# X, Z and V of a long convolution: planes moved between partitions inside SBUF, V summed by TensorE, keys set aside and spread later

## What is computed

```python
dtA = exp(log_dt) * (-exp(log_A_real) + 1j * A_imag)          # (256, 64)
Ct = C * (exp(dtA) - 1) / A
K = 2 * real(einsum('hn,hnl->hl', Ct, exp(dtA[:, :, None] * arange(1024))))
y = irfft(rfft(x, n=2048) * rfft(K, n=2048).T)[:, :1024]      # long convolution
x = layernorm(x + layernorm_affine(x + y + x * D))
x = layernorm(x + cross_attention(x, ctx))                    # 16 heads of 16
x = layernorm(x + dense_gate(x) + experts(x))                 # 4 heads, 8 of 1024 experts
```

## Time and profile before

| | us |
|---|---|
| median of 3 runs | 710.08 (703.44 to 712.31) |
| profiled execution, own time | 702.58 |
| its span, first to last instruction | 700.8 |
| first matmul of `conv` after the start | 188.22 |
| busy: TensorE, VectorE, ScalarE, GpSimd | 590.3, 506.6, 404.9, 279.9 |

### The profile page before, as it was taken

How to read it: one execution, slowest core, us unless ns; L and a number is a source line. 1 busy time by engine, 2 the same in 40 slices (tenths; PEclk the granted TensorE clock), 3 DMA queues, 4 the chain that set the end, 5 groups by cost and what they waited for, 6 DMA issues and landing times.

```text
span 700.8 us, 9712 instructions
## 1 busy us (share of the span) xinstructions
PE 590.3 (84%) x3132; PEld 383.4 (55%) x3132; DVE 506.6 (72%) x1046; ACT 404.9 (58%) x593; POOL 279.9 (40%) x333
## 2 busy tenths in 40 slices
PE   5743587785296778999999999999999999899996
PEld 2512366563264554445678565478575479453485
DVE  7999985523047885898866879767778797578783
ACT  4971655222042435797763878675579765577760
POOL 0002871635041345543343634235635234644361
PEclk9876989898596567999999999999999999999999
DMA  8945030456325000000000000000000000000000
GB/s 239 363 204 91 1 98 2 119 162 144 89 83 217 1 1 1 0 1 0 1 1 0 17 8 7 1 1 1 9 8 8 8 1 1 8 16 7 0 8 23
DMA packets 20111, 34.27 MB, mean 49 GB/s; under 512 B 7388, under 2 KB 14045, under 8 KB 18333
## 3 DMA queue, kind: packets, MB, share of 16 engines
q1 hardware_dynamic: 15677, 29.46, 13.7%
q10 hardware_dynamic: 4384, 4.20, 2.0%
HBM read 21.94 MB, written 10.65 MB: 47 GB/s over the span
## 4 chain that ended last, share of the span: by engine, by line
PE 60%; DVE 22%; ACT 7%; issue 6%; POOL 3%; DMA 1%; SPq 0%; ACTq 0%; DVEq 0%; POOLq 0%
PE banks L773 20%; PE banks L863 8%; PE banks L868 7%; PE banks L818 4%; PE banks L840 3%; PE banks L795 3%; PE banks L830 3%; PE banks L804 2%; PE banks L715 2%; DVE stats L1377 2%; ACT arena L882 2%; PE banks L651 2%; DVE arena L1468 2%; PE banks L855 2%; ACT arena L1067 1%
## 5 line engine op out<-in xcount | busy, mean ns | idle before, releaser
L1169 POOL TENSOR_TENSOR arena<-arena 128x1024 f32<-128x1024 f32 x64 | 125.8, 1965 | 156.6 <-ACT arena L1067 155.6
L773 PE MATMUL banks<-arena 128*128 128x512 f32 x384 | 174.6, 596 | 5.4 <-issue 3.7
L773 PEld LDWEIGHTS banks<-arena 128*128 128x128 f32 x384 | 69.9, 190 | 83.2 <-issue 76.5
L1067 ACT ACTIVATE arena<-arena 128x1024 f32<-128x1024 f32 x64 | 73.5, 1149 | 7.5 <-DVE arena L1466 3.2
L1069 ACT ACTIVATE arena<-arena 128x1024 f32<-128x1024 f32 x64 | 73.5, 1149 | 2.1
L1468 DVE SCALAR_TENSOR_TENSOR arena<-arena 128x1024 f32<-128x1024 f32 x48 | 63.8, 1329 | 1.7
L863 PE MATMUL banks<-arena 128*128 128x256 f32 x256 | 58.4, 381 | 2.4 <-DVE tok L1504 1.2
L957 ACT COPY arena<-banks 128x512 f32<-128x512 f32 (+1 forms) x64 | 34.1, 532 | 44.8 <-PE banks L765 29.3
L868 PE MATMUL banks<-arena 128*128 128x256 f32 x256 | 57.9, 379 | 0.0
L1142 POOL TENSOR_SCALAR arena<-mv 128x1 f32<-128x1 f32 (+1 forms) x40 | 14.1, 353 | 105.2 <-DVE mv L1378 103.8
L971 ACT ACTIVATE tok<-tok,arena,rstd 128x256 f32<-128x256 f32 x48 | 27.9, 598 | 45.5 <-POOL arena L1147 44.6
(11 more groups left out here) (179 smaller groups left out, 1077.4 us busy)
## 6 DMA issues: line engine op xcount, KB each, us to landing
scr_x<-arena SPq DMA_DIRECT2D x16, 256.0 KB, 3.2
arena<-scr_x SPq DMA_DIRECT2D x2, 2048.0 KB, 13.8
arena<-scr_z SPq DMA_DIRECT2D x32, 128.0 KB
scr_z<-arena ACTq DMA_DIRECT2D x14, 256.0 KB, 7.1
tok<-in_x SPq DMA_DIRECT2D x8, 256.0 KB, 5.7
out<-tok SPq DMA_DIRECT2D x16, 128.0 KB, 1.7
arena<-in_imat SPq DMA_DIRECT2D x1, 1152.0 KB, 5.6
arena<-in_fmat SPq DMA_DIRECT2D x1, 1088.0 KB, 7.0
```

The lines of the kernel that those rows point to most:

```text
L773: ins = mm(bk[:, :], w[:, k, P * m:P * m + P], src[:, k, :], start=(k == 0), stop=(k == KC - 1))
L1067: fn(ebuf[m % 2], sxb[m % 2], ACT.Prelu, bias=negt[:, n % 2, h:h + 1], alpha=FAR).then_inc(s_ranked, 1)
L1169: tt(sxb[m % 2], sim[:, n % 2, h, 0:XR].unsqueeze(2).broadcast_to((P, XR, NKEYS)), sim[:, n % 2, FH + h, :].unsqueeze(1).broadcast_to((P, ...
```

## The change

- **X**: the 16 DMAs out of cA write straight into xS, eight partitions each, without scr_x. fmat is loaded ahead of them, ctxT, wk and wv lie elsewhere. All nine `x_second` stand ahead of `taps(0)` in the order of TensorE, in two pairs of banks (0, 1 and 4, 5).
- **Z**: SP copies each plane from zring to zB as soon as ScalarE has filled the slot, without scr_z; ScalarE issues no DMA for it. zring has three slots instead of four. The columns of imat are in another order so that the 128 partitions match. The inverse has two sets of banks from its fifth step on.
- **V**: VectorE and GpSimd leave the two terms of V side by side (v_terms; the factors are ordered so that they add), and TensorE sums them: 64 matmuls for each group instead of 32. Groups alternate between banks 0, 1 and 4, 5.
- **Keys and values**: ScalarE sets keys and values aside (`stage`), the bias of the values is added by a one-row matmul, VectorE spreads the keys late (`keys`, after table 6).
- **Orders**: due times moved. ScalarE has `x_second` 0 ahead of `simw`; GpSimd has spectra 0 ahead of the second `skip`, `values` and `x_bias` later. In the main part VectorE has two of four `pair` steps of one tile in four ahead of an `inner` step; the other engines' orders there are the same.

```diff
-ZRING = 4
+ZRING = 3
+Z_NARROW = 4
...
-         "ln_steps": (-0.336, -0.234, 0.162, 0.013, 0.361), "sines": (-3.002, -2.884), "tables": (0.0,),
-         "taps": (0.982,), "x_second": (-0.756, 0.69), "skip": (0.382,), "k_first": (5.96, 0.01, 9.6, 0.059),
-         "simw": (-1.866,), "x_bias": (2.891, 0.086), "values": (2.518,), "diagonal": (-1.627,),
-         "k_second": (7.974, 0.1, 9.65, 0.1), "spectra": (7.989999999999999, 0.1, 9.67, 0.1),
-         "inverse": (8.27, 0.1, 9.9, 0.12), "products": (0.0, 1.0, 0.0, 0.996, 0.0, 0.802, -0.084, 0.975),
+         "ln_steps": (-0.336, -0.234, 0.162, 0.013, 0.361), "sines": (-2.96, -2.46), "tables": (-0.035,),
+         "taps": (0.977,), "x_second": (-2.2, 0.25), "skip": (1.02,), "k_first": (5.965, 0.01, 9.581, 0.059),
+         "simw": (-2.144,), "x_bias": (2.952, 0.541), "values": (3.224,), "stage": (-2.504,), "keys": (6.605,),
+         "diagonal": (-1.627,), "k_second": (7.974, 0.1, 9.65, 0.1), "spectra": (7.989999999999999, 0.14, 9.67, 0.1),
+         "inverse": (8.356, 0.092, 9.853, 0.113), "products": (0.0, 1.0, 0.0, 0.996, 0.0, 0.802, -0.084, 0.975),
...
-       ("dve", "expert"): 0.129, ("dve", "inner"): 0.049, ("dve", "outer"): 0.141, ("dve", "spread"): 0.104,
+       ("dve", "expert"): 0.129, ("dve", "inner"): 0.078, ("dve", "outer"): 0.141, ("dve", "spread"): 0.1,
+       ("act", "first"): 0.034, ("dve", "taps"): -0.042, ("pool", "project"): -0.002}
...
-    imat = imat.reshape(P, FREQ, 2, 2, NQ, NS).transpose(0, 1, 2, 3, 5, 4).reshape(P, FREQ, 2, P)
+    imat = imat.reshape(P, FREQ, 2, 2, NQ, NS).transpose(0, 1, 2, 5, 3, 4).reshape(P, FREQ, 2, P)
...
 
-        cross_terms = part("cross_terms", o_tab + 4096, 2, CH, HALF)
+        v_terms = [part(f"v_terms{d}", at, 2, CH, HALF) for d, at in enumerate((o_tab + 4096, o_par))]
...
+        def x_bank(m):
+
+            return 4 * (m % 2)
+
+        def group_bank(g):
+
+            return 4 * (g % 2)
+
         def z_bank(m):
 
-            return 2 * (m % 2) if m >= FREQ else 0
+            return 2 * (m % 2) if m >= Z_NARROW else 0
...
             for dst, n in ((ctxT, "ctxT"), (wk, "wk"), (wv, "wv"), (pcol[:, :], "pcol")):
                 sp.dma_start(dst, t[n]).then_inc(s_ctx, 16)
+            sp.dma_start(rows[0:1, 4, :], t["rows"][0:1, 4, :]).then_inc(s_ctx, 16)
+            sp.dma_start(fmat, t["fmat"]).then_inc(s_mat, 16)
             sp.dma_start(wqf, t["wqf"]).then_inc(s_wsim_in, 16)
             sp.dma_start(keysT, t["keysT"]).then_inc(s_wsim_in, 16)
 
             for q in range(NQ):
                 sp.wait_ge(s_xae, 2 * (q + 1))
                 for h in range(2):
-                    sp.dma_start(scr_x[q % QUAD, q // QUAD, h].rearrange("s r n -> (s r) n"),
-                                 cA[:, h, q, :]).then_inc(s_xaw, 16)
-            for dst, n in ((rows[:, :, :], "rows"), (head_mask[:, :], "head_mask"), (value_mask, "value_mask")):
+                    p0 = NS * (4 * (q % QUAD) + 2 * (q // QUAD) + h)
+                    sp.dma_start(xS[p0:p0 + NS, 0:NSLOT, :], cA[:, h, q, :]).then_inc(s_xaw, 16)
+            sp.dma_start(rows[:, 0:4, :], t["rows"][:, 0:4, :]).then_inc(s_rows, 16)
+            for dst, n in ((head_mask[:, :], "head_mask"), (value_mask, "value_mask")):
                 sp.dma_start(dst, t[n]).then_inc(s_rows, 16)
-            sp.dma_start(fmat, t["fmat"]).then_inc(s_mat, 16)
-            sp.wait_ge(s_xaw, 16 * 2 * NQ)
-            sp.wait_ge(s_cm, 4)
-            for h in range(2):
-                sp.dma_start(xS[:, 8 * h:8 * h + 8, :].rearrange("p r n -> p (r n)"),
-                             scr_x[:, :, :, :, 8 * h:8 * h + 8, :].rearrange("a b c s r n -> (a b c s) (r n)")).then_inc(
-                                 s_xb[h], 16)
             sp.wait_ge(s_kbz, 1)
             sp.dma_start(t["scr_v"].rearrange("b h k d -> k (b h) d"),
                          vaug.rearrange("k b h d -> k (b h) d")).then_inc(s_vw, 16)
...
             sp.wait_ge(s_ktm, 2 * NGRP)
             for n in range(2 * FREQ):
                 hf, k = divmod(n, FREQ)
+                sp.wait_ge(s_ze, n + 1)
+                for j, r in enumerate(tiles_of(k)):
+                    sp.dma_start(zB[NS * r:NS * r + NS, hf].rearrange("s h q n -> s (h q) n"),
+                                 zring[:, n % ZRING, j, :]).then_inc(s_zw[n % ZRING], 16)
+
+            for n in range(2 * FREQ - ZRING, 2 * FREQ):
                 sp.wait_ge(s_zw[n % ZRING], 16 * z_writes(n + 1, n % ZRING))
-                for r in tiles_of(k):
-                    sp.dma_start(zB[NS * r:NS * r + NS, hf].rearrange("s h q n -> s h (q n)"),
-                                 scr_z[hf, r].rearrange("(h s q) n -> s h (q n)", h=2, s=NS)).then_inc(s_zr[hf], 16)
-
...
                 ins.then_inc(s_cm, 1)
             for b in range(B):
                 for ic in range(KC):
-                    ins = mm(bank[4 + b][0:NKV, D:2 * D], ctxT[:, ic, NKV * b:NKV * b + NKV], wv[:, ic, :],
-                             start=(ic == 0), stop=(ic == KC - 1))
-                ins.then_inc(s_cm, 1)
+                    mm(bank[4 + b][0:NKV, D:2 * D], ctxT[:, ic, NKV * b:NKV * b + NKV], wv[:, ic, :],
+                       start=(ic == 0), stop=False)
+                if b == 0:
+                    pe.wait_ge(s_ones, 1)
+                mm(bank[4 + b][0:NKV, D:2 * D], vaug[0:1].rearrange("k b h d -> k (b h d)")[:, 0:NKV], bv[0:1],
+                   start=False, stop=True).then_inc(s_cm, 1)
...
 
                 pe.wait_ge(s_tab, g + 1)
                 pe.wait_ge(s_utab, g + 1)
-                if g:
-                    pe.wait_ge(s_kev, 2 * g)
+                if g >= 2:
+                    pe.wait_ge(s_kev, 2 * g - 2)
+                b0 = group_bank(g)
                 v, u = power[g % 2]
+                sums = [(c, table) for c in range(2) for table in (v, v_terms[g % 2])]
                 for k in range(CH // 4):
                     f = slice(4 * k, 4 * k + 4)
                     for half in range(2):
                         modes = slice(64 * half, 64 * half + 64)
-                        for c in range(2):
-                            ins = mm(bank[4 + half][:, P * k:P * k + P], u[modes, c, f, :].rearrange("p f a -> p (f a)"),
-                                     v[modes, c, f, :].rearrange("p f a -> p (f a)"),
-                                     start=(c == 0), stop=(c == 1), skip_group_check=True)
+                        for j, (c, table) in enumerate(sums):
+                            ins = mm(bank[b0 + half][:, P * k:P * k + P], u[modes, c, f, :].rearrange("p f a -> p (f a)"),
+                                     table[modes, c, f, :].rearrange("p f a -> p (f a)"),
+                                     start=(j == 0), stop=(j == 3), skip_group_check=True)
                         if k == CH // 4 - 1:
                             ins.then_inc(s_ktm, 1)
 
...
 
             def x_second(k1):
                 pe.wait_ge(s_mat, 16)
-                for h in range(tiles_of(k1)[-1] // 8 + 1):
-                    pe.wait_ge(s_xb[h], 16)
-                if k1:
-                    pe.wait_ge(s_xfe, k1)
-                second_stage(k1, bank[0], bank[1], lambda r: xS[:, r, :]).then_inc(s_xf, 1)
+                pe.wait_ge(s_xaw, 16 * 2 * NQ)
+                b0 = x_bank(k1)
+                if k1 > 1:
+                    pe.wait_ge(s_xfe, k1 - 1)
+                elif k1 == 1:
+                    pe.wait_ge(s_kbz, 1)
+                second_stage(k1, bank[b0], bank[b0 + 1], lambda r: xS[:, r, :]).then_inc(s_xf, 1)
...
                 m = FREQ * hf + k
                 pe.wait_ge(s_imat, 16)
                 pe.wait_ge(s_xfe, FREQ)
+                pe.wait_ge(s_kev, 2 * NGRP - 2)
                 pe.wait_ge(s_yf, m + 1)
-                if m > FREQ:
-                    pe.wait_ge(s_ze, m - 1)
-                elif m:
-                    pe.wait_ge(s_ze, m)
+                if m >= Z_NARROW:
+                    pe.wait_ge(s_tab, NGRP)
+                if m:
+                    pe.wait_ge(s_ze, m - 1 if m > Z_NARROW else m)
...
             for kind, n in order(HEAD, "pe"):
                 if kind == "taps":
                     if n == 0:
-                        pe.wait_ge(s_kbd, 1)
                         pe.wait_ge(s_kbz, 1)
+                        pe.wait_ge(s_xfe, FREQ)
...
-            src = bank[4 + i % 2][:, :].rearrange("p (k c) -> p c k", c=P)
+            src = bank[group_bank(g) + half][:, :].rearrange("p (k c) -> p c k", c=P)
...
                         act.wait_ge(s_cm, 5 + k)
                         nc.scalar.copy(wsim[:, k, :], bank[2 + k][:, :]).then_inc(s_ce, 1)
                         own.done(s_ce)
+                elif kind == "stage":
+
+                    act.wait_ge(s_cm, KC + B)
+                    act.wait_ge(s_ctx, 16 * 5)
+                    for oc in range(KC):
+                        fn(kstage[:, oc, :], bank[4 + oc][:, 0:B * NKV], ACT.Identity,
```

(59 more changed lines are left out.)

## The result

The changed kernel is slower: 745.9 us (median of 4 runs, 737.9 to 752.5) against 706.8 (4 runs, 701.2 to 712.3), a ratio of 1.054 with a 95% interval of 1.038 to 1.071. The forecast of 696 us and its range up to 715 missed it. The profiled execution has a span of 735.4 us, 34.6 more than the earlier trace rows.

A forecast was written before the change was run, and what follows sets the result against it. Bound: the stretch before conv, with Z's round trip through HBM idling TensorE 18.8 us. Inverse 9 at 155.5 plus 21.6 put conv at 177 against 188.2; 707.1 - 11.2 = 696 us, range 675 to 715.

The forecast's parts named there:

- the price of a copy into eight partitions: Copies of X and Z inside SBUF: 119 GB/s, 1.1 us for 128 KB and 2.2 us for 256 KB.
- the half rate: Rival, chance 0.13: copies of X and Z at 60 GB/s, X at 88, conv at 236, span 755 us.
- the port rule: Copies into eight neighbours: bandwidth follows ports reached, two ports, an estimated 54 GB/s, 2.4 us for 128 KB; conv near 250.
- The second near row: SBUF-to-SBUF transfer of the taps before the change, 14.0 GB/s per engine, taken as 112 GB/s on eight engines.
- The lower bound of 60 GB/s: Lowest rate allowed for copies into eight partitions, set at half of the near rows.
- both hindrances at once: Short pieces out of SBUF and one partition per engine together, shown by no row; argued for 60 GB/s.
- The order behind X: Head: late X holds up x_second, simw and powers(1); X at 54, powers(1) at 60.8, taps 0 at 75.7.
- Tables and taps: Stage before the inverses: 64 matmuls in 4.2 us per group, taps 7 ends at 126, inverse 0 at 129.
- The keys: VectorE's 3.5 us of keys fall into its wait for taps 5 (108.7 to 112.8) and cost nothing.
- Half 1: First nine inverse steps, with two copies of 2.2 us per step: end at about 145.4, inverse 9 at 155.5.
- the fast rival: Rival, chance 0.22: copies at 26 GB/s per engine, X at 38, conv at 158, gain 30, 677 us.
- The main part: From conv on, only VectorE's order changes, eight swaps of a 1.33 us instruction: 0, with 3 us each way.

The follow-up runs named there:

- the series: Kernel before, unchanged, with timed copies of known shape behind its last output; 1.05 MB into eight neighbouring partitions took 19.2 to 20.5 us.
- X alone spread: Changed kernel with the copies of X into eight partitions 4 apart, those of Z still into eight neighbours: 1.007, span 703.8 us.
- Z alone spread: Changed kernel with the copies of Z into eight partitions 4 apart, those of X still into eight neighbours: 1.008, span 708.9 us.
- its reads spread: Kernel before with its 32 reads of Z from HBM landing in eight partitions 4 apart instead of eight neighbours: 0.985, span 691.4 us.
- the second set: Kernel before, unchanged, with further copies behind its last output to map the ports; four neighbours took 0.52 MB in 18.4 us.
- both spread: Changed kernel with the copies of X and of Z into eight partitions 4 apart: 678.5 us, 0.961.

## Why the prediction was wrong

**The failed step is the price of a copy into eight partitions**: 119 GB/s taken (1.1 us for 128 KB), 62 (Z, 2.1 us) and 76 (X) measured, 55 in the series with its start and 62 while it runs. From 177 to 221.9 us the start of `conv` slipped by 44.9, in three pieces that all come from it: X at 73.3 and not at 54, and so inverse 0 at 147.9 and not at 129 (18.9 us); inverse 9 (183.4) 35.5 us behind inverse 0 and not 26.5 (9.0); `conv` 38.5 us behind inverse 9 and not 21.6 (16.9). The runs bear the pieces out: with X alone spread inverse 0 is at 117.7, and with Z alone spread inverse 9 is 24.8 us behind inverse 0 and `conv` 19.1 behind that. The rival that happened is the half rate, held at 0.13: X at 88, `conv` at 236 and 755 us were a little too dark, since X ran at 76.

**How it failed.** One window was taken for the rate of the reads, 178 to 185 us. The DMA view of the kernel before for 166 to 170 us, in the same reads, says:

```profile
q1 hardware_dynamic: 50, 0.28, 52.3%
```

0.28/(0.523 x 16 x 4) = 8.4 GB/s for each engine, half of the 16.1 in the earlier trace rows. ScalarE's writes run beside the reads there, but they don't explain it: in the same window of the kernel before with its reads spread, beside more writes, the reads have

```profile
q1 hardware_dynamic: 74, 0.40, 30.0%
```

or 0.40/(0.30 x 16 x 4) = 20.8 GB/s for each engine. With both windows of the kernel before side by side the trace would have asked why one form has two rates, and could not have been said to speak against the port rule of the Trainium skill (SBUF — State Buffer, section Door 1: The DMA port swizzle). The forecast put that rule aside with "The trace of before doesn't agree"; for two ports the series bear it out. Its estimate of `conv` near 250 was 28 us too late, most of it in X, at 76 GB/s where the estimate from that rule was 54. Why X ran faster in the kernel than the 53 GB/s of its own form in the series (L626; 59 without the start) is not shown. The second near row, the taps at 112 GB/s, goes to 32 neighbours; the same form in the second set (L639) took 0.52 MB in 4.2 us. It was no row for eight. The lower bound of 60 GB/s came out near the 62 measured by luck: it was argued from "both hindrances at once" and not from the targets. The row to look for was one whose targets reach as few ports.

**The order behind X** held: TensorE's `x_second`, ScalarE's `simw`, `powers(1)` 6.4 us behind X (6.8 forecast), first taps 19.6 us behind X (21.7 forecast), inverse 0 74.6 us behind X (75; with X at 44.9 it was 76.2). That the last agrees so well is part luck: the taps start 2.1 us sooner behind X than forecast, and the stage behind them takes 1.7 us longer.

**Tables and taps.** The matmuls were mis-sized: 64 take 5.04 us, not 4.2 (from 125.96 to 131.00 in the timeline), 79 ns each, at the same granted clock of 1.0. It cost some 2 us on the path: first taps to last 52.3 us (92.89 to 145.15) against 50.3. TensorE's wait for GpSimd's table 4 was 2.64 us and not 4.7. The keys took 3.30 us in VectorE's wait, at no cost.

**Half 1 and the end without the narrow copies**: with both spread, inverse 9 (145.9) is 24.8 us behind inverse 0 (26.5 forecast) and `conv` 19.2 us behind that (21.6). The terms around the price were good to 2.4 us. That both spread reach 678.5 us, where the fast rival had 677, is in part chance: that rival had X at 38 and `conv` at 158, and measured are 44.9 and 165.1; and it counted from a mean of 707.1 us for the kernel before, where the runs beside both spread have a median of 705.8.

**The main part** was counted at 0 and came out 0.9 us longer.

## What to carry to other kernels

A copy between partitions is priced by its bytes and by the ports that its narrow side reaches, not by the length of its pieces or by where its source lies; before such a copy is added, choose the partitions (4 apart in a block of 32) and let the constants absorb the permutation. When a trace must stand for an operation that isn't in it, look at every window of the nearest row and not at one; two rates for one form are a question to settle first. A slow transfer can hide the worth of the rest of a change: with Z through HBM the inverses were over 7 us earlier, and `conv` started 0.8 us earlier.

## What the runs showed of the hardware

- In series of 0.5 to 1 MB with some 2 us of start included, eight neighbouring partitions take 50 to 55 GB/s whatever the piece (0.5 to 4 KB), four take 28; eight partitions 16 apart take 84, 4 apart 114 to 130. The same holds for a narrow source (54) and for HBM on the other side (48 to 60). While the stream runs, four, eight neighbours, eight 16 apart and eight 4 apart take 31, 62, 101 and 173.
- Inside a kernel the rate into eight neighbours was 62 (copies of Z), 76 (copies of X) and, in one window of 7 us, 126 GB/s (reads of Z); what raises it there is open.
- A single read of 128 KB into eight neighbours takes 3.7 to 4.1 us from issue to landing.
- Copies to planes 32 partitions apart in turn are the slowest (21.6 us for 1.05 MB, against 19.4 for far halves; one series each).
